# The down projection's low-rank A appended to the streamed down weights, in place of matmuls of its own

## What is computed

```python
x = x + 0.5 * ffn(layernorm(x))
x = x + s4(layernorm(x))
x = x + 0.5 * ffn(layernorm(x))      # the same weights

def qlinear(x, q, scale, A, B):      # q: integers 0..15
    w = (q - 7.5) * (scale * 0.005)[:, None]
    return x @ w.T + 0.02 * (x @ A @ B)     # A, B have rank 32

def ffn(x):                          # 512 -> 1376 -> 512
    h = silu(qlinear(x, gate...)) * qlinear(x, up...)
    return qlinear(h, down...)
```

## Time and profile before

| | |
|---|---|
| three runs | 631.31, 631.45 and 633.48 us; median 631.45 |
| profiled execution | span 632.9 us, from its first to its last instruction; the page gives no other time of it |
| TensorE (PE) busy | 601.7 us, 95% of the span |
| VectorE (DVE) busy | 457.9 us, 72% |
| ScalarE (ACT) busy | 270.9 us, 43% |
| GpSimd (POOL) busy | 72.3 us, 11% |
| mean granted TensorE clock | 0.992 |

### The profile page before, as it was taken

The page is one execution under the profiler, slowest core; times in us unless marked ns, Lnnn a source line. Parts: engine busy times, 40 slices in busy tenths (PEclk is TensorE's granted clock), DMA queues, the critical chain, the costliest instruction groups (busy, mean ns, idle before and its releaser), DMA issues.

```text
span 632.9 us, 9273 instructions
## 1 busy us (share of the span) xinstructions
PE 601.7 (95%) x3070; PEld 290.9 (46%) x3070; DVE 457.9 (72%) x851; ACT 270.9 (43%) x505; POOL 72.3 (11%) x89
## 2 busy tenths in 40 slices
PE   3798899999999999999997999999999999999997
PEld 2443444444444545444454544444454444544443
DVE  6699949895788868793698589548874688556643
ACT  3765303662066404561563366216640565126620
POOL 4236800000000001000064000000000000000000
PEclk9999989999999999999997999999999999999999
DMA  8984120004000210000278000300031001250001
GB/s 298 395 279 132 39 46 1 2 1 76 8 0 0 50 33 2 1 1 2 49 140 141 21 2 1 75 9 2 1 55 29 0 0 27 56 200 0 1 9 59
DMA packets 67620, 35.46 MB, mean 56 GB/s; under 512 B 56160, under 2 KB 60448, under 8 KB 67584
## 3 DMA queue, kind: packets, MB, share of 16 engines
q1 hardware_dynamic: 66768, 34.87, 21.0%
q10 hardware_dynamic: 816, 0.14, 0.1%
HBM read 17.43 MB, written 4.19 MB: 34 GB/s over the span
## 4 chain that ended last, share of the span: by engine, by line
PE 79%; DVE 8%; issue 1%; ACT 1%; DVEq 1%; ACTq 0%
PE bank L1047 41%; PE bank L1025 22%; PE bank L1004 5%; PE bank L1065 5%; PE bank L981 2%; PE bank L1144 2%; PE bank L1126 1%; PE bank L1013 1%; DVE z L627 1%; DVE work L708 1%; DVE zs L620 1%; DVE X L670 1%; DVE X L911 1%; DVE uq_raw L667 0%; DVE z L629 0%
## 5 line engine op out<-in xcount | busy, mean ns | idle before, releaser
L512 ACT ACTIVATE work<-bank,scales 128x512 f32<-128x512 f32 (+1 forms) x176 | 120.3, 684 | 173.8 <-PE bank L1047 173.3
L1047 PE MATMUL bank<-xT,gw 128*128 128x512 f16 (+1 forms) x696 | 164.4, 379 | 0.8 <-ACT work L512 0.8
L1047 PE MATMUL bank<-xT,uw 128*128 128x512 f16 (+1 forms) x696 | 164.4, 379 | 0.0
L1025 PE MATMUL bank<-dw,hT 128*128 128x512 f16 (+1 forms) x704 | 160.6, 381 | 0.0
L1047 PEld LDWEIGHTS bank<-xT,gw 128*128 128x128 f16 (+1 forms) x696 | 69.4, 100 | 81.2 <-ACT work L512 1.6
L1047 PEld LDWEIGHTS bank<-xT,uw 128*128 128x128 f16 (+1 forms) x696 | 69.7, 100 | 79.8
L1025 PEld LDWEIGHTS bank<-dw,hT 128*128 128x128 f16 (+1 forms) x704 | 68.1, 98 | 78.6 <-issue 2.2
L690 DVE SCALAR_TENSOR_TENSOR work<-bank,work 128x512 f32<-128x512 f32 (+1 forms) x88 | 60.6, 688 | 27.2 <-ACT work L512 21.3
L703 DVE SCALAR_TENSOR_TENSOR work<-bank,work 128x512 f32<-128x512 f32 (+1 forms) x88 | 60.4, 686 | 20.8 <-ACT work L512 20.4
L708 DVE TENSOR_TENSOR work<-work 128x512 f32<-128x512 f32 (+1 forms) x88 | 63.7, 724 | 4.7 <-ACT work L535 1.3
L648 DVE SCALAR_TENSOR_TENSOR hT<-work,hT 128x512 f16<-128x512 f32 (+1 forms) x88 | 61.2, 695 | 6.1 <-ACT hT L517 5.6
(11 more groups left out here) (145 smaller groups left out, 436.7 us busy)
## 6 DMA issues: line engine op xcount, KB each, us to landing
out_x<-X SPq DMA_DIRECT2D x16, 256.0 KB, 2.1
X<-in_x SPq DMA_DIRECT2D x1, 2048.0 KB, 14.8
gq_raw<-in_tables SPq DMA_DIRECT2D x1, 2048.0 KB, 11.7
gq_raw<-in_gate_q_t SPq DMA_DIRECT2D x2, 768.0 KB, 11.3
uq_raw<-in_up_q_t SPq DMA_DIRECT2D x2, 768.0 KB, 11.3
dq_raw<-in_down_q_t SPq DMA_DIRECT2D x1, 1536.0 KB, 14.6
work<-in_b SPq DMA_DIRECT2D x2, 688.0 KB, 8.4
X<-in_x SPq DMA_DIRECT2D x4, 256.0 KB, 5.3
```

Of the source, the lines that this page charges most:

```text
L512: return nc.scalar.activation(out, in_, ACT.Copy, scale=scales[0:rows[m], g, m:m + 1])
L1025: last = mm(bank[4 + b][:, :], hT[0:rows[m], m, a, j * P:(j + 1) * P], dw[0:rows[m], m, :], start=(m == 0 and a == 0), stop=(m == M - 1 an ...
L1047: last = mm(dst[0:r, :], w[:, c, cols], xT[:, a, c, :], start=(c == 0 and a == 0), stop=(c == KH - 1 and a == 1))
```

## The change

The stationary operand of the down passes, an hT block, is also what Pd needs. The change appends A (32 columns for its high half, 32 for its low one) to the first 256 down weight columns, so that a sub-tile's product becomes two passes over hT: c = 0 with 320 columns (256 outputs and the 64 of Pd) and c = 1 with the other 256. Each pass has 22 matmuls. The two halves lie in the two PSUM banks of down_acc[j % 2]; down_low moves to bank 2. Pd now comes out with rows on partitions, so each sub-tile's goes through ScalarE (pd_high, three reads of 32 columns), VectorE (pd_split), a transpose on TensorE (pd_transpose, into bank 3) and a copy on ScalarE (pd_copy) to PdT. The orders of the queues change with it. TensorE for each j: pass 0; p_product(n+1, j); blocks 0 to 8 of pass 1; pd_transpose; blocks 9 and 10 of pass 1; down_low. ScalarE for each j: pd_high, pd_copy, p_high(n+1, j). VectorE for each j: pd_split, p_split(n+1, j), down_read, down_add. The first low_rank(0) of a tile also waits for the last sum of the tile before.

```diff
-        bank = [ctx.enter_context(nc.psum_tensor(f"bank{i}", [P, 512], F32)) for i in range(8)]
+        bank = [ctx.enter_context(nc.psum_tensor(f"bank{i}", [P, 512], F32)) for i in range(4)]
+        down_acc = [ctx.enter_context(nc.psum_tensor(f"down_acc{b}", [P, 2, 512], F32)) for b in range(2)]
+        bank += [down_acc[b][:, h, :] for b in range(2) for h in range(2)]
...
-        dw = sb("dw", [P, M, H], F16)
+        HH = H // 2
+        HALF = HH + 2 * R
+        dw = sb("dw", [P, M, 2, HALF], F16)
         a_w = sb("a_w", [P, KH, 4 * R], F16)
-        da_w = sb("da_w", [P, M, 4, R], F16)
...
+        pd_stack = sb("pd_stack", [P, 2, 4, R], F16)
...
-        c_bank = [bank[4], bank[5], bank[2], bank[3]]
+        c_bank = bank[4:8]
...
-            def pd_high(n):
-
-                act.wait_ge(f.pd_mm, n + 1)
-                after(act, f.dl_mm, n * TS)
-                nc.scalar.activation(PdT[:, :], bank[0][:, :], ACT.Copy,
-                                     scale=1.0 / (H_SCALE * A_SCALE)).then_inc(f.pd_hi, 1)
+            def pd_high(n, j):
+
+                k = n * TS + j
+                act.wait_ge(f.pd_mm, k + 1)
+                after(act, f.pd_t, k - 1)
+                for slot, col in ((0, 0), (3, 0), (2, R)):
+                    last = nc.scalar.activation(pd_stack[:, j % 2, slot, :], down_acc[j % 2][:, 0, HH + col:HH + col + R],
+                                                ACT.Copy, scale=1.0 / (H_SCALE * A_SCALE))
+                last.then_inc(f.pd_hi, 1)
+
+            def pd_copy(n, j):
+
+                act.wait_ge(f.pd_t, n * TS + j + 1)
+                after(act, f.dl_mm, n * TS + j)
+                nc.scalar.activation(PdT[:, j * P:(j + 1) * P], bank[3][:, 0:P // 2].bitcast(F16), ACT.Copy)\
+                    .then_inc(f.pd_out, 1)
...
-                pd_high(n)
-                if more:
-                    for j in range(TS):
+                for j in range(TS):
+                    pd_high(n, j)
+                    pd_copy(n, j)
+                    if more:
                         p_high(n + 1, j)
+                    if s4 and j == 1:
+                        act.wait_ge(s_toep, 1)
+                        nc.scalar.activation(toep[:, :], bank[0][:, :], ACT.Copy).then_inc(s_tcopy, 1)
+                    if s4 and j == 2:
+                        for i in range(2):
+                            conv_norm(i)
                 if s4:
-                    act.wait_ge(s_toep, 1)
-                    nc.scalar.activation(toep[:, :], bank[2][:, :], ACT.Copy).then_inc(s_tcopy, 1)
-                    for i in range(AHEAD):
+                    for i in range(2, AHEAD):
                         conv_norm(i)
...
-            def pd_split(n):
-                dve.wait_ge(f.pd_hi, n + 1)
-                V.scalar_tensor_tensor(PdT[R:2 * R, :], bank[0][R:2 * R, :], 1.0 / (H_SCALE * A_SCALE),
-                                       PdT[R:2 * R, :], ALU.mult, ALU.subtract).then_inc(f.pd_out, 1)
+            def pd_split(n, j):
+                dve.wait_ge(f.pd_hi, n * TS + j + 1)
+                V.scalar_tensor_tensor(pd_stack[:, j % 2, 1, :], down_acc[j % 2][:, 0, HH:HH + R],
+                                       1.0 / (H_SCALE * A_SCALE), pd_stack[:, j % 2, 0, :],
+                                       ALU.mult, ALU.subtract).then_inc(f.pd_stack, 1)
...
-                V.tensor_tensor(dtmp[:, b, :], bank[4 + b][:, :], d_scale[:, :], ALU.mult)\
+                V.tensor_tensor(dtmp[:, b, :].rearrange("p (c h) -> p c h", c=2), down_acc[b][:, :, 0:HH],
+                                d_scale[:, :].rearrange("p (c h) -> p c h", c=2), ALU.mult)\
...
-                pd_split(n)
-                if more:
-                    p_split(n + 1, 0)
-                    p_split(n + 1, 1)
-                down_read(n, 0)
-                if more:
-                    p_split(n + 1, 2)
-                down_add(n, 0, base)
-                if more:
-                    p_split(n + 1, 3)
-                down_read(n, 1)
-                down_add(n, 1, base)
+                for j in (0, 1):
+                    pd_split(n, j)
+                    if more:
+                        p_split(n + 1, j)
+                    down_read(n, j)
+                    down_add(n, j, base)
                 if s4:
                     s4_diagonal()
                     s4_maximum()
-                    for i in range(TS):
-                        conv_low(i)
-                        if i == 1:
-                            s4_split()
                 if isinstance(n, int) and n == 0:
                     s4_vectors()
                     s4_inverse(0)
                 for j in (2, 3):
+                    pd_split(n, j)
+                    if more:
+                        p_split(n + 1, j)
                     down_read(n, j)
                     down_add(n, j, base)
+                    if s4 and j == 2:
+                        s4_split()
+                        conv_low(0)
+                        conv_low(1)
+                if s4:
+                    conv_low(2)
+                    conv_low(3)
...
-                for slot in (0, 1, 3):
-                    hi = V.tensor_scalar(da_w[:, :, slot, :], da_raw, A_SCALE, None, ALU.mult)
-                hi.then_inc(s_dhi, 1)
+                V.tensor_scalar(dw[:, :, 0, HH:HH + R], da_raw, A_SCALE, None, ALU.mult).then_inc(s_dhi, 1)
                 dve.wait_ge(s_dhi, 2)
-                V.scalar_tensor_tensor(da_w[:, :, 2, :], da_raw, A_SCALE, da_w[:, :, 0, :],
+                V.scalar_tensor_tensor(dw[:, :, 0, HH + R:HALF], da_raw, A_SCALE, dw[:, :, 0, HH:HH + R],
                                        ALU.mult, ALU.subtract).then_inc(s_dw, 1)
...
-            def pd_product(n, half):
-
-                if half == 0:
-                    pe.wait_ge(f.tg[(M - 1) % 2], uses(n, M - 1) + 1)
-                    pe.wait_ge(f.hlo[0], uses(n, M - 3) + 1)
-                    pe.wait_ge(f.hlo[1], uses(n, M - 4) + 1)
-                for m in (range(0, DQ), range(DQ, M))[half]:
-                    if m >= M - 2:
-                        pe.wait_ge(f.hlo[m % 2], uses(n, m) + 1)
+            def h_ready(n, m):
+
+                if m in (0, 1):
+                    pe.wait_ge(f.hlo[m], uses(n, M - 3 - m) + 1)
+                if m >= M - 2:
+                    pe.wait_ge(f.hlo[m % 2], uses(n, m) + 1)
+
+            def down_pass(n, j, c, blocks):
+
+                b, width = j % 2, (HALF, HH)[c]
+                if c == 0 and blocks[0] == 0:
+                    after(pe, f.d_read[b], n * 2 + j // 2)
+                for m in blocks:
+                    if j == 0 and c == 0:
+                        h_ready(n, m)
+                        if isinstance(n, int) and n == 0:
+                            pe.wait_ge(s_dcast, m + 1)
                     for a in range(2):
-                        last = mm(bank[0][:, :], da_w[0:rows[m], m, :, :].rearrange("p a r -> p (a r)"),
-                                  hT[0:rows[m], m, a, :], start=(m == 0 and a == 0),
+                        last = mm(down_acc[b][:, c, 0:width], hT[0:rows[m], m, a, j * P:(j + 1) * P],
+                                  dw[0:rows[m], m, c, 0:width], start=(m == 0 and a == 0),
                                   stop=(m == M - 1 and a == 1))
-                if half:
-                    last.then_inc(f.pd_mm, 1)
+                if blocks[-1] == M - 1:
+                    last.then_inc((f.pd_mm, f.d_mm[b])[c], 1)
+
+            def pd_transpose(n, j):
+
+                pe.wait_ge(f.pd_stack, n * TS + j + 1)
+                after(pe, f.pd_out, n * TS + j)
+                nc.tensor.transpose(bank[3][:, 0:P // 2].bitcast(F16),
+                                    pd_stack[:, j % 2, :, :].rearrange("p a r -> p (a r)"), ident16[:, :])\
+                    .then_inc(f.pd_t, 1)
 
             def down_low(n, j):
-                pe.wait_ge(f.pd_out, n + 1)
+                pe.wait_ge(f.pd_out, n * TS + j + 1)
                 after(pe, f.dsum, n * TS + j)
-                mm(bank[6][:, :], PdT[:, j * P:(j + 1) * P], db_w[:, :], start=True, stop=True)\
+                mm(bank[2][:, :], PdT[:, j * P:(j + 1) * P], db_w[:, :], start=True, stop=True)\
                     .then_inc(f.dl_mm, 1)
-
-            def down_half(n, j, half):
-
-                b = j % 2
-                if half == 0:
-                    after(pe, f.d_read[b], n * 2 + j // 2)
-                for m in (range(0, DQ), range(DQ, M))[half]:
-                    if j == 0 and isinstance(n, int) and n == 0:
-                        pe.wait_ge(s_dcast, m + 1)
-                    for a in range(2):
-                        last = mm(bank[4 + b][:, :], hT[0:rows[m], m, a, j * P:(j + 1) * P],
-                                  dw[0:rows[m], m, :], start=(m == 0 and a == 0),
-                                  stop=(m == M - 1 and a == 1))
-                if half:
-                    last.then_inc(f.d_mm[b], 1)
...
```

(58 more changed lines are left out.)

19 lines of the change are left out of this document (11 added, 8 removed).

## The result

| | before | after |
|---|---|---|
| median of the runs, us | 632.28 | 644.57 |
| lowest to highest (4 runs each) | 631.31 to 633.48 | 643.84 to 646.26 |
| ratio, 95% interval | | 1.0189 [1.0161, 1.0216] |
| span of the profiled execution | 632.9 | 642.1 |

The forecast was 643.7. First the page of the kernel after, part 1 (busy time, share, instructions) and the first line of part 4 (the chain that ended last, by engine), beside the earlier trace rows.

What follows compares the result with a forecast made beforehand. TensorE, busy 95%, was taken as the bound: in six of eight sections removed columns come off the time and waits add to it. 5×0.1 + 6.6 − 0.7 + 2.8 + 3.0 = 12.2 on 631.45 gave 643.7, range 635 to 652.

Steps and rivals of the forecast that it cites:

- The saving, 1.96 a tile: Down sections: 22 matmuls of 512 columns removed, passes of 2.99 and 2.40; 1.96 saved a tile, 15.7 in all.
- Steps 1 and 2: First sub-tile: TensorE waits 0.82 for h's last block, every tile, and 0.83 for the first transpose's split, with a next tile.
- Step 3: Before each down_low, TensorE waits 0.11 for ScalarE's copy of PdT, 32 times (bounds 0.05 and 0.21).
- Step 4: Tile boundaries: low_rank(0) waits 1.10 for the next tile's low-rank factors to land, at six boundaries, 6.6 in all.
- Step 5: Tile 0's section: waits for h and splits, +1.2 at full clock; with one half-clock stretch, +2.8 (range +1.2 to +4.4).
- Step 6: Tile 3 and convolution: conv_low work shares VectorE's queue with pd_split, so the convolution's chain ends later, +3.0 (+1 to +5).
- ScalarE's cast of uw holds the same block, so nothing is gained: First tile: down_a writes one copy instead of three on VectorE, claimed to gain nothing because of ScalarE's cast.
- ready matmuls behind it: Rival: ready matmuls pass a waiting transpose or down_low, so plain waits hide and the time is 623.5; 8 in 100.
- The landing did not come in time: Rival it answers: factors land 1.2 after the DMA issue, boundaries cost nothing, time 637.1; 7 in 100.
- clock of 1.00: Rival it answers: the clock falls in every section, 1.6 for seven of them, time 655; 5 in 100.
- The widths kept their rate: Rival it answers: narrow matmuls miss the column rate, 256-column ones taking 136 ns, 19 more, 663; 2 in 100.

Runs made afterwards that it cites:

- the control: The kernel before, unchanged, run and profiled a second time: 632.93 us, span 631.2.
- p_high first: Kernel after, with ScalarE making p_high(n+1, j) before pd_copy(n, j) instead of after it: 636.63 us, ratio 1.0072 to the kernel before.
- low-rank later: Kernel after, with the gate's low-rank product behind the up product in every tile's first block on TensorE: 637.58 us, ratio 1.0075 to before.
- order of tile 3: Kernel after, tile 3 only: pd splits 2 and 3 ahead of VectorE's convolution work, ScalarE's first two conv norms sooner: 639.35 us, ratio 1.0096.
- more copies: Kernel after, with VectorE again making scaled copies of A in the first tile, two operations more, results overwritten: 646.27 us, ratio 1.0201 to before.
- h covered: Kernel after, with twelve second-pass matmuls put ahead of the last blocks of h in sub-tile 0: 645.38 us, ratio 1.0202 to before.
- all five and tile 0: Kernel after with five order edits together, plus pd splits 0 and 2 moved earlier on VectorE in tile 0: 616.44 us, ratio 0.9752 to before.
- all but h: Kernel after with four order edits together, sub-tile 0's first pass again running straight through to block 10 of h: 623.99 us, ratio 0.9869 to before.
- split first: Kernel after, with VectorE's pd_split(n, 0) between the next tile's two ln_apply instead of behind both: 639.86 us, ratio 1.0123 to before.

## Why the prediction was right

The forecast of 643.7 was 0.9 below the median, and the kernel was slower for the reasons given. That the sum came so near is in part luck. The prediction has 0, +3.9, +6.0, +3.0 and −0.7 for the start, tile 0, the five plain boundaries, tile 3 with the convolution, and tile 7; measured against the control these are −0.9, +1.4, +6.7, +4.5 and −0.8. Two parts were put too high and two too low, and the errors cancel. By its steps:

- **The saving, 1.96 a tile.** Confirmed: passes of 2.99 and 2.40, and 1.86 less in the plain tiles once almost nothing waits. Narrow matmuls kept the column rate: the 6.12 of a sub-tile is the sum of its columns' times with nothing left over. From the Trainium skill ("TensorEngine Tiling (Array Packing)", Instruction Overhead) I had worked out an estimate of 25 ns for each further instruction. The 6.12 has no room for it, so the measurement decides against that rule here.
- **Steps 1 and 2, 0.82 and 0.83.** From start to start 0.83 and 0.70; the split takes 0.18, where I put 0.22 at most. The mechanism holds, and so does their sum as the length of a section (26.4 in the trace, 169.79 + 0.22 − 143.59, where I put 26.5). What the sum did not say is that they stand in series: taking away the first alone gives nothing, the second alone 0.7.
- **Step 3, 0.11 for the copy.** 0.10; the copy takes 0.28, as estimated between two neighbours of other widths.
- **Step 4, 1.10 at six boundaries.** The mechanism is confirmed from two sides, "p_high first" and "low-rank later". The size is 1.28 at five of them and 1.72 at 4, 5, where the last landing took 2.8. Counted from the last transpose, low_rank(0) starts 3.82 later where I put 3.65. With the sections the five plain boundaries cost 6.7 where my sum has 6.0.
- **Step 5, tile 0, +2.8.** With the boundary 3.9 for tile 0 to 1. Measured is +1.4 in the kernel after and +3.1 in "order of tile 3" and "more copies", whose tile 0 has the same order. With the half clock off its path, as in the kernel after, its section is 0.3 longer than before where I put 1.2: the third transpose waited 2.1 for its split, not 2.7. A pass at the half clock adds 1.7 in two of these three profiles and nothing in the first. The mechanism holds, and the size was put too high.
- **Step 6, tile 3 and the convolution, +3.0.** Measured +3.1 against the first profile and +4.5 against the control, which had less of the half clock. The first marks came: conv_low(3) ends 37.7 after T0 (forecast 37.8) and the fifth addition 46.2 (46.2). One row was misread: 325.47 is the end of GpSimd's conv_low(8), and conv_low(7) ended at 321.16, 37.0 after T0. So conv_low(7) is 7.0 later in the kernel after (44.0), not 2.9, and conv_low(8) 5.1 later. GpSimd's rstd for tile 4's layer-norm stands behind it and starts 4.3 later (46.3 for 42.0), and the next pair of additions ends 4.4 later (52.7 for 48.4), near the +4.5. That the order of the queues in tile 3 is the cause, the edit shows; whether VectorE's or ScalarE's, it does not.
- **Wrong: "ScalarE's cast of uw holds the same block, so nothing is gained".** VectorE's copies set the start of the section, and two copies fewer were worth about 1 us. It is small, and its sign is against the others: the sum with it would be 11.2.

The rivals are out. TensorE stood at the first transpose of each plain tile with ready matmuls behind it. The landing did not come in time at any of the six boundaries. The down sections of the plain tiles have a clock of 1.00. The widths kept their rate.

## What to carry to other kernels

A change that saves columns on a TensorE that is busy 95% is worth its columns only if each new dependence has cover, that is, ready work of the engine ahead of its wait. Cover shrinks with the saving: the shorter first pass (2.72 for 4.3 up to the last block) is itself what made TensorE wait for h. Write down, for each engine's strict queue, what a new small operation stands behind; here five small changes of order decide between +1.9% and −2.3%. And test edits together as well as alone: waits in series hide each other, and an edit that shows nothing alone can be worth 0.7 a tile once its neighbour is gone. Read the length of a wait from start to start: a bracket of the timeline fell 0.16 short here.

## What the runs showed of the hardware

**The half clock can be free or not, and this varies between executions of kernels that are alike up to there.** The table by stretch (length, PE busy, granted clock, DMA share, GB/s) of the kernel after and of "more copies":

```profile
74.00:76.00 2.00, 2.00 (x13) 0.53 0.03 8
76.00:78.00 2.00, 1.91 (x10) 0.61 0.25 51
78.00:80.00 2.00, 1.97 (x15) 1.00 0.43 80
```

```profile
78.00:80.00 2.00, 1.09 (x8) 1.00 0.68 131
80.00:82.00 2.00, 2.00 (x11) 0.59 0.15 33
82.00:84.00 2.00, 2.00 (x11) 0.56 0.68 130
```

In the first the half clock (1.2 GHz) came 1.1 after the end of the pause of 1.84 for h, and took time that TensorE would have spent waiting for the split: the transpose starts 9.79 after T0 in both kernels. In the second two pauses of 1.85 and 1.78 went by before it fell, and it lay on a pass on the path: 4.67 for 2.99. That is the 1.7 by which tile 0 differs (77.02 to 75.34). "Order of tile 3", which has the kernel after's order up to there, went the second way as well, so the difference is not one of the copies. In "h covered" two pauses, of 3.08 and 1.88, were each followed by the half clock (0.50 from 78 to 80 and 0.65 from 94 to 96). In "all five and tile 0" pauses of 0.54 and 1.06 were followed by none, nor were two of 1.85 in "all but h". Why it falls behind some of these pauses and not behind others of the same length, these runs do not show.

**A landing is not always 2.3.** Of the 28 transposing DMAs into PT in each run, the slowest took 3.9 in the kernel after; it was not the last of a boundary, and TensorE did not wait for it. The last one at 4, 5 took 2.8, and that boundary was 0.44 longer than the others. In "split first" one issue took 2.21 for 1.17, and from down_low to low_rank(0) its boundary took 4.28 where 1, 2 took 3.23. A boundary that has just enough cover by the median has none for these.
